# Attention: one exponential over four banks a step, four heads' scores in one stretch

## The reference, cut to what matters

```python
scores = jnp.einsum('bhqd,bhkd->bhqk', q, k) * scale
scores = jnp.where(causal[None, None], scores, -jnp.inf)
attn = jax.nn.softmax(scores, axis=-1)
out = jnp.einsum('bhqk,bhkd->bhqd', attn, v)
```

## Time and profile before

| what | us |
|---|---|
| median of 3 runs | 14266.07 (14263.33 to 14268.62) |
| the profiled execution | 14259.61, its span 14257.8 |
| TensorE busy, share of the span | 6236.3, 44% |
| VectorE busy | 10111.8, 71% |
| ScalarE busy | 8230.9, 58% |
| GpSimd busy | 865.8, 6% |

### The profile page before, as it was taken

How to read it: one execution, slowest core, us unless ns; L and a number is a source line. 1 busy time by engine, 2 the same in 40 slices (tenths; PEclk the granted TensorE clock), 3 DMA queues, 4 the chain that set the end, 5 groups by cost and what they waited for, 6 DMA issues and landing times. The chain is left out here.

```text
span 14257.8 us, 225375 instructions
## 1 busy us (share of the span) xinstructions
PE 6236.3 (44%) x52114; PEld 4468.0 (31%) x52114; DVE 10111.8 (71%) x54778; ACT 8230.9 (58%) x42355; POOL 865.8 (6%) x821
## 2 busy tenths in 40 slices
PE   7222222222222222222222222224678655588997
PEld 5222222222222222222222222223444444343335
DVE  3777777777777777777777777776386388627851
ACT  4666666666666666666666666665265211123661
POOL 0000000000000000000000000000000066411000
PEclk9555555555555555555555555555699677798998
DMA  1101001000010010100100001000000000001100
GB/s 44 19 13 19 13 13 19 13 18 13 13 19 13 13 19 13 19 13 13 19 13 17 15 13 19 13 13 13 11 1 1 18 5 0 6 34 39 30 17 18
DMA packets 339189, 226.33 MB, mean 16 GB/s; under 512 B 27349, under 2 KB 324001, under 8 KB 337702
## 3 DMA queue, kind: packets, MB, share of 16 engines
q1 hardware_dynamic: 337958, 213.24, 7.0%
HBM read 187.35 MB, written 25.43 MB: 15 GB/s over the span
## 5 line engine op out<-in xcount | busy, mean ns | idle before, releaser
L515 PE MATMUL scan_p_car<-scan_hs,scan_mean_mat 32*32 32x2 f32 x16392 | 577.6, 198 | 6860.4 <-DVE scan_hb L642 6848.1
L515 PEld LDWEIGHTS scan_p_car<-scan_hs,scan_mean_mat 32*32 32x32 f32 x16392 | 401.8, 135 | 7039.3 <-DVE scan_hb L642 7026.9
L560 ACT ACTIVATE scan_act_ps<-scan_act_ps 128x64 f32<-128x64 f32 (+1 forms) x8193 | 1641.8, 200 | 64.6
L560 ACT ACTIVATE scan_act_ps<-scan_r 128x64 f32<-128x64 f32 x2048 | 466.2, 228 | 1870.8 <-DVE scan_r L639 1870.8
L542 PE MATMUL scan_p_y<-scan_c_masked,scan_hb 128*64 128x4 f32 x16384 | 1234.2, 253 | 0.0
L520 PE MATMUL scan_p_car<-scan_eps_row,ones 1*128 1x3 f32 x4102 | 1197.9, 360 | 38.7 <-DMA scan_a_log<-L_attn_a_A_log 38.5
L560 ACT ACTIVATE scan_cm<-scan_dl,scan_s 128x64 f32<-128x64 f32 x2049 | 712.3, 348 | 737.0 <-DVE scan_s L665 737.0
L639 DVE TENSOR_TENSOR scan_c<-scan_V,scan_cm 128x64 f32<-128x64 f32 x4096 | 740.5, 221 | 459.9 <-ACT scan_cm L560 412.1
L542 PEld LDWEIGHTS scan_p_y<-scan_c_masked,scan_hb 128*64 128x64 f32 x16384 | 1055.4, 216 | 34.3
L520 PEld LDWEIGHTS scan_p_car<-scan_eps_row,ones 1*128 1x128 f32 x4102 | 1020.4, 308 | 71.4 <-DMA scan_a_log<-L_attn_a_A_log 38.9
L642 DVE SCALAR_TENSOR_TENSOR scan_uw<-scan_w,scan_rsq 128x64 f32<-128x64 f32 x2048 | 460.3, 225 | 660.1 <-ACT scan_rsq L560 654.6
(11 more groups left out here) (452 smaller groups left out, 19344.0 us busy)
## 6 DMA issues: line engine op xcount, KB each, us to landing
scan_step_in<-scan_scratch SPq DMA_DIRECT2D x520, 256.0 KB, 6.1
qk_scratch<-qkv_parts SPq DMA_DIRECT2D x32, 384.0 KB, 2.5
attn_qT<-qk_scratch SPq DMA_DIRECT2D x192, 64.0 KB, 2.2
attn_kT<-qk_scratch SPq DMA_DIRECT2D x192, 64.0 KB, 2.2
scan_scratch<-prep_dts SPq DMA_DIRECT2D x32, 256.0 KB, 2.1
x<-L_attn_a_x SPq DMA_DIRECT2D x1, 4096.0 KB
out<-x SPq DMA_DIRECT2D x1, 4096.0 KB
filter_taps<-c_kT SPq DMA_DIRECT2D x1, 2048.0 KB
```

What stands on the lines that cost most here:

```text
L515: last = nc.tensor.matmul(p_car[slot][rows, 0:2], mean_mat[rows, :], hs[rows, :], start=False, stop=True)
L560: nc.scalar.activation(dst, src, func, **kw).then_inc(counts[par]["act"], 1)
```

## The change

A step's four heads are handled together. `scores` does all four heads in one call and waits for the whole exponential of the step before; one ACTIVATE reads four banks and writes a `pT` buffer of four heads, of which there are two; `s_done` and `exp_done` count steps where they counted pairs. TensorE's order is now scores, the first part of the pieces, the value products of the step before, all other pieces.

```diff
-        pT = [ph.sb(f"pT{k}", [P, 2, GT]) for k in range(4)]
+        pT = [ph.sb(f"pT{k}", [P, HG, GT]) for k in range(2)]
...
-                            sp.wait_ge(s_done, it * STEP_PAIRS + 2 * (FIRST_OF_HEAD[h] - FETCH_AHEAD))
+                            sp.wait_ge(s_done, it * len(STEPS) + FIRST_OF_HEAD[h] - FETCH_AHEAD)
...
-                def scores(it, n, pair):
+                def scores(it, n):
...
-                        pe.wait_ge(exp_done, it * STEP_PAIRS + 2 * n + pair - 1)
-                    for h in (2 * pair, 2 * pair + 1):
+                        pe.wait_ge(exp_done, it * len(STEPS) + n)
+                    for h in range(HG):
...
-                    pe.wait_ge(exp_done, it * STEP_PAIRS + 2 * n + 2)
+                    pe.wait_ge(exp_done, it * len(STEPS) + n + 1)
...
-                        last = nc.tensor.matmul(ps[h * VW:(h + 1) * VW, SUM_BANK, off:], vs[it % 2][:, kt, h, :], pT[(2 * n + h // 2) % 4][:, h % 2, off:],
+                        last = nc.tensor.matmul(ps[h * VW:(h + 1) * VW, SUM_BANK, off:], vs[it % 2][:, kt, h, :], pT[n % 2][:, h, off:],
...
-                        scores(it, n, 0)
+                        scores(it, n)
                         for u in places[0]:
-                            piece(it + 1, u)
-                        scores(it, n, 1)
-                        for u in places[1]:
                             piece(it + 1, u)
                         if n:
                             values(it, n - 1)
                         elif it:
                             values(it - 1, len(STEPS) - 1)
-                        for u in places[2] + places[3]:
+                        for u in places[1] + places[2] + places[3]:
                             piece(it + 1, u)
...
-                        for pair in range(2):
-                            act.wait_ge(s_done, 2 * step + pair + 1)
-                            if step >= 2 and pair == 0:
-                                act.wait_ge(pv_done, step - 1)
-                            nc.scalar.activation(pT[(2 * n + pair) % 4][:, :, off:], ps[:, 2 * pair:2 * pair + 2, off:], ACT.Exp).then_inc(exp_done, 1)
+                        act.wait_ge(s_done, step + 1)
+                        if step >= 2:
+                            act.wait_ge(pv_done, step - 1)
+                        nc.scalar.activation(pT[n % 2][:, :, off:], ps[:, 0:HG, off:], ACT.Exp).then_inc(exp_done, 1)
```

More of the change, by code:

```diff
@@ L2148, in attention_phase @@
     STEPS = [(c, kt) for c in range(CHUNKS) for kt in range(GP * (c + 1))]
-    STEP_PAIRS = 2 * len(STEPS)
     PIECES = [(h, j, n) for h in range(HG) for j in range(TB) for n in range(0, (j + 1) * P, GT)]
@@ L2255, in _ @@
                     if it:
-                        sp.wait_ge(s_done, it * STEP_PAIRS)
+                        sp.wait_ge(s_done, it * len(STEPS))
                     for h in range(1, HG):
                         if h > 1:
-                            sp.wait_ge(s_done, it * STEP_PAIRS + 2 * (FIRST_OF_HEAD[h] - FETCH_AHEAD))
+                            sp.wait_ge(s_done, it * len(STEPS) + FIRST_OF_HEAD[h] - FETCH_AHEAD)
                         load(it + 1, h)
                     if it + 2 < GROUPS:
-                        sp.wait_ge(s_done, it * STEP_PAIRS + 2 * (FIRST_OF_HEAD[HG - 1] + FETCH_AHEAD))
+                        sp.wait_ge(s_done, it * len(STEPS) + FIRST_OF_HEAD[HG - 1] + FETCH_AHEAD)
                         load(it + 2, 0)
```

## The result

| | before | after |
|---|---|---|
| median, us | 14268.62 (14263.33 to 14272.25, 5 runs) | 14335.74 (14326.22 to 14340.68, 5 runs) |
| ratio | | 1.0046, 95% interval 1.0032 to 1.0061 |
| span of the profiled execution | 14257.8 | 14333.9 |
| ScalarE busy in the span | 8230.9 | 8208.5 |
| seven groups, first exponential to first exponential | 765.17 | 805.66 |

The change makes the kernel 67 us slower; 14331 was forecast, with the range 14294 to 14374. From the start of attention's first exponential to the start of the last step's (of its first half, where there are two), the trace shows 843.87 us before and 913.47 after: +69.6. The profiled span grew by 76.1, 6.5 more, because attention started 8.1 us later (13012.44 against 13004.30) and 1.6 was made up behind it.

The account below looks back on a forecast made before the run. Seven groups were taken as paced by TensorE, VectorE close behind, the eighth by ScalarE; merged, an exponential-scores chain sets the floor. +27.8 (eighth) and +36.8 (seven) gave +64.6 us, 14331 us, range 14294 to 14374.

Parts of the forecast that it names:

- The new chain: Every attention step: exponential, scores, exponential without overlap, 3.00 us for a full step, a floor of 108.5 us a group.
- The eighth group: Last group, without pieces: 106.5 us from first to last exponential against 78.7, a cost of +27.8 us.
- The seven groups: Groups that also look for the next group's maxima: 114.7 us each, +36.8 us for all seven.
- Turned sums: Transposes of the sums at each chunk's second step wait for a bank behind the value products: +3.2 us a group.
- Five- and six-piece steps: Sixteen full steps a group with five or six pieces, taken as 3.10 us each: +1.6 us a group.
- Step 36: Where transposed maxima wait for VectorE, whose reads come one read later: +0.7 us a group.
- less 1 us: Group 0, which has no sums to turn in its first chunk: 1 us off the seven groups' cost.
- The floor alone: Rival, 10%: the seven groups take only the chain's 108.5 us each; +22 us in all, 14288 us.
- The falling clock: Rival, 5%: TensorE drops to 1.2 GHz in the eighth group, about 34 us more, 14365 us.
- A faster exponential: Rival, 2%: one operation over four banks takes about 1.3 us, making the kernel faster, 14247 us.
- a granted clock under 1.00: Sign in the eighth group that the prediction listed as showing it wrong.
- The rule: Skill's advice that grouping helps a saturated engine: eighth group would gain 1.6 us, total +35, 14301 us; forecast rejected it.

Follow-up runs that it names:

- e1: Changed kernel with its exponential cut into two 1024-element operations, every wait still counting whole steps: ratio 1.0066, attention 925.03 us, a group 116.14, eighth group 110.11.
- e2: Kernel before, keeping its pair waits, with only TensorE's order of the change: ratio 1.0005, attention 857.56 us, a group 110.54, eighth group 78.68.
- e10: Changed kernel run again unaltered: ratio 1.0054, attention 913.84 us, a group 114.83, eighth group 110.35.
- e3: Changed kernel with value products behind the first two parts of the pieces instead of the first: ratio 1.0049, attention 903.62 us, a group 113.08, eighth group 109.24.
- e4: Changed kernel with TensorE's old order, pieces between the two score pairs: ratio 1.0074, attention 958.45 us, a group 121.41, eighth group 107.75.
- e5: Kernel before with both score pairs in one stretch, value products behind two parts of pieces as before: ratio 1.0003, attention 849.39 us, a group 109.15.
- e6: e5 with the turned sums put ahead of the value products: ratio 0.9999, attention 859.26 us, a group 110.76, eighth group 78.75.
- e7: e2 with the turned sums put ahead of the value products: ratio 0.9999, attention 854.45 us, a group 110.20, eighth group 78.75.
- e9: Kernel before with its pieces spread over steps 0 to 34 instead of 35: ratio 1.0008, attention 852.22 us, a group 110.40, eighth group 78.68.
- e8: Changed kernel with three unused 512-column matmuls after each step's value products in the eighth group: one run, attention 916.06 us, eighth group 110.06.

## Why the prediction was right, point by point

**The new chain** held. Full step 3.01 us measured for 3.00; the four widths as priced; 1.88 + 0.05 + 1.03 + 0.04 can be read off after's timeline to 0.01. e1 and e2 show its cause from both sides: with two operations and one wait the loss stays, with the change's order and two waits it goes, wholly in the eighth group and but for 13.7 us over attention.

**The exponential** (-9 to +9 us, taken as 1.88) measured 1877 ns.

**The eighth group**: +27.8 forecast, +29.1 measured. Leaving out what the low clock added to single steps (0.61 + 0.41), after's is 106.79 us long, against 106.5 forecast. e10 less its 3.57, e3 less 2.45 and e4 less 0.96 come to 106.79 as well. Where after's first and eighth group begin and where the last exponential starts (timeline of ScalarE):

```profile
13012.44 1.88 ACT L2421 ACTIVATE attn_pT<-attn_ps 128x2048 f32<-128x2048 f32 x1 [6.20 <-PE attn_ps L2345]
...
13818.10 1.88 ACT L2421 ACTIVATE attn_pT<-attn_ps 128x2048 f32<-128x2048 f32 x1 [1.45 <-PE attn_ps L2345]
...
13925.91 0.60 ACT L2421 ACTIVATE attn_pT<-attn_ps 128x512 f32<-128x512 f32 x1 [0.73 <-PE attn_ps L2345]
```

**The seven groups**: 114.7 forecast, 114.83 measured in each of groups 2 to 6. By parts, each as the steps' excess over the same kind of step in the eighth group:

- Turned sums: +3.2 forecast; 1.06 + 0.61 + 0.62 + 1.02 = +3.3. After's timeline of such a step, 4.07 us long, shows the bank wait:

```profile
13602.92 0.82 PE L2323 MATMUL attn_ps<-attn_kT,attn_qT 96*128 96x512 bf16 x3
...
13603.35 1.29 DVE L2455 TENSOR_REDUCE attn_top_pieces<-attn_ps 128x1 f32<-128x512 f32 x2 [0.26 <-PE attn_ps L2323]
13604.16 0.42 PEld L2367 LDWEIGHTS attn_ps<-ident,attn_o_sum 128*128 128x128 f32 x4 [0.91 <-issue]
13604.19 0.63 PE L2367 MATMUL attn_ps<-ident,attn_o_sum 128*128 128x128 f32 x4 [0.44 <-DVE attn_top_pieces L2455]
```

From the first piece to the transposes it is 1.27 us, for the 1.17 that the prediction put together from the earlier trace rows.
- Five- and six-piece steps: +1.6 forecast, +1.4 measured, but not spread evenly. Most full steps cost nothing over 3.01; step 19 costs 0.62 (3.87 against 3.25), and steps 28 and 29 cost 0.65 together. That the estimate of 3.10 for each of 16 came near the sum is luck.
- Narrow steps: +0.7 forecast, +1.0.
- Step 36: +0.7 forecast, +0.3. This term was too large; the step is 0.26 us longer, not by a whole read of 0.6.

**The sum of seven** is +40.5 where +36.8 was forecast. The term that was mis-sized is group 0, "less 1 us": it took 116.65 in this profile where 113.7 was forecast. Its first steps ran at the lower clock, which the term had put at nothing though the kernel before, too, begins attention at 0.50 (13004.30 to 13009.50):

```profile
13012.40:13023.50 11.10, 10.88 (x64) 4.16 (x62) 7.13 (x21) 4.95 (x4) 0.00 (x0) 0.65 0.11 31
13023.50:13040.00 16.50, 15.48 (x96) 5.11 (x94) 14.03 (x33) 9.87 (x6) 0.00 (x0) 1.00 0.00 0
```

(windows of after). Its steps 0 and 1 take 3.86 and 4.41 us, in e10 3.03 and 2.49: 2.75 more. In e10 the group is 113.91, 0.92 under its neighbours, which is the forecast "less 1". The remaining 1.0 us is 0.13 a group, 114.83 against 114.7.

**The total.** That 14335.74 lies within 5 us of 14331 says less than it seems: the ratio's interval is 20 us to each side, the baseline's median had moved by 2.6 us, and within attention the profiles show 5 us more than the sum of +64.6 (69.6; e10 70.0). The terms above, not the median, bear the forecast out.

**The rivals.** The floor alone (108.5 a group) is excluded by 114.83: the bank wait of the turned sums did sit ahead of the next scores. The falling clock was right in kind and wrong in size: the clock does fall in the eighth group, but for 3.4 us at a time and not for all of it, so it costs 1.0 us (after, e1, e4) to 3.6 (e10) and not 34. A faster exponential is excluded by 1877 ns. The prediction had called "a granted clock under 1.00" there a sign of being wrong. The sign came (0.98), and the forecast stood all the same, so the sign was too sharp.

**The rule.** ScalarE's busy time fell by 29 us over attention, and attention became 69.6 us longer. The Trainium skill, Perfetto Trace Analysis, Optimizing Scalar/DVE Operations, ties grouping to a saturated engine, and says that breaking instructions up may help where the engine isn't saturated but others wait for it. The runs agree with the second half only where the waits are broken up too: with pair waits again attention is 55.9 us shorter (e2 against after), while e1, which breaks up the operation alone, is 11.6 us longer. For the eighth group, where ScalarE was 86% busy and the prediction read 1.6 us of gain out of the first half, the trace shows +29.1: the engine was near full because its input came in two halves. With the same operations and one wait (e1) it is busy 68.6 of 110.2 us.

**Size of the two parts.** Of the 69.6 us the new order with pair waits accounts for 13.7 (e2) and the merge with its one wait for 55.9, 29.1 in the eighth group and 26.8 in the others. But the parts depend on each other: with pair waits the new order costs 1.95 us a group, and once the merge is there it spares 6.8 (121.6 to 114.8).

## What to carry to other kernels

Before joining two operations that take turns over buffers, ask which producer filled one buffer while the consumer read the other; if the joined operation covers all buffers, step time becomes consumer plus producer plus hand-overs (here 1.88 + 1.03 + 0.09) and the busy share that argued for joining was a product of the halves. Forecast such a chain first where nothing else is in play (here the last group), then add for each other stretch only what its busiest engine has beyond it. Where several users take turns over few banks, ask what the producer does while the consumer reads: the value products (1.00 us) hide a read where they stand between a piece and the next user of its bank (e5), and hide nothing where they stand ahead of both (after) or behind both (e6).

## What was not expected of the hardware

- **Short falls of TensorE's clock.** In the eighth group with one wait a step, the granted clock is at 0.50 for about 3.4 us at a time, once in after, e1 and e4 (e4: 0.90 over 17 us), twice in e3, three times in e10. Each adds 1.0 to 1.5 us: only the matmuls on the chain count, and exponentials keep their 1.88. The kernels with pair waits (before, e2, e5, e6, e7, e9) show 1.00 throughout it. The places have something in common: every one of these eight falls begins at most 1.3 us from the end of TensorE's longest idle time there, 1.61 us (1.67 in e1), which comes in the first step of a chunk, where TensorE has only the 128-wide value products (0.43 us) before it waits. e5 has one such fall outside the eighth group (13446.80 to 13450.20 at 0.50), 1.7 us behind an idle time of 1.61 us that its scores spent waiting for the rows' DMAs; it makes group 4 of e5 1.2 us longer. In the eighth group of e8 no idle time of TensorE is above 0.9 us, and there is no fall. Twelve of the twenty places of this kind in the five profiles see none, and which do differs between two profiles of the same kernel; that stays open.
- **The spread of the start.** Attention's first exponential lies between 12996.56 (e9) and 13059.96 us (e2) in these profiles, with the work ahead of it unchanged. A single span is no measure of a change of this size. The stretch's own length came to 913.47 and 913.84 in two profiles of the changed kernel, though in parts that differ by up to 2.7 us.
- **The exponential's duration stays on one line up to four banks**, as the prediction took it to, from widths of two banks and less: 597, 1024, 1451 and 1877 ns for 512 to 2048 elements, 0.83 ns an element and 0.17 us fixed.
